# A transformer layer with eight experts: the matmuls of each expert get three widths chosen at run time, some adds of the prefix-sum step move to GpSimd, and the routing step gets a second buffer

## The reference, cut to what matters

```python
# attention part: prefix sums over time, no softmax
k_real = xn @ Wk;  v = xn @ Wv
k = exp(1j * 10 * k_real);  rotors = exp(1j * t * freqs)
out = gate0 * real(cumsum(v * rotors) * conj(rotors)) / sqrt(t + 1)
    + gate1 * real(cumsum(v * conj(k shifted by one token)) * k) / sqrt(t + 1)
attn = out @ Wo
# expert part: every token goes to the one expert with the largest probability
probs = softmax(xn @ gate_w);  e = argmax(probs)
ffn = probs[e] * (gelu(xn @ w1[e] + b1[e]) @ w2[e] + b2[e])      # 1024 -> 4096 -> 1024
```

## Time and profile before

| | |
|---|---|
| median of 3 runs | 1149.34 us (1148.93 to 1155.68) |
| the profiled execution | 1152.25 us; its slowest core's span 1150.4 us |
| spans of the eight cores | 1135.3 to 1150.4 us, the longest is core 4 |
| busy on core 4 | PE 932.1, PEld 611.9, DVE 756.4, ACT 598.4, POOL 162.6 us |
| instructions on core 4 | 18743 |
| HBM read, written by core 4 | 321.18 MB, 17.90 MB |

### The profile page before, as it was taken

How to read it: one execution, slowest core, us unless ns; L and a number is a source line. 1 busy time by engine, 2 the same in 40 slices (tenths; PEclk the granted TensorE clock), 3 DMA queues, 4 the chain that set the end, 5 groups by cost and what they waited for, 6 DMA issues and landing times.

```text
span 1150.4 us, 18743 instructions; the slowest of 8 cores (1135.3 to 1150.4 us)
## 1 busy us (share of the span) xinstructions
PE 932.1 (81%) x6221; PEld 611.9 (53%) x6296; DVE 756.4 (66%) x1909; ACT 598.4 (52%) x1014; POOL 162.6 (14%) x184
## 2 busy tenths in 40 slices
PE   3756689699989999988889978987898784978592
PEld 2323456465656666656556646654665462544261
DVE  4726444756645546689976998999989995321331
ACT  4354477668875795576347634873377422210000
POOL 0000121001112111121012101210121110311101
PEclk9876689999989999999899988998899887988896
DMA  8999999995999999999999999999999999999982
GB/s 190 228 204 205 203 158 172 163 158 106 164 139 160 181 179 162 159 174 169 159 176 170 169 156 175 173 163 159 159 164 167 158 156 196 210 230 217 203 230 79
DMA packets 123779, 199.69 MB, mean 174 GB/s; under 512 B 4755, under 2 KB 70691, under 8 KB 123680
## 3 DMA queue, kind: packets, MB, share of 16 engines
q0 software_dynamic: 107056, 151.65, 88.8%
q1 hardware_dynamic: 16624, 46.80, 12.6%
HBM read 321.18 MB, written 17.90 MB: 295 GB/s over the span
## 4 chain that ended last, share of the span: by engine, by line
PE 33%; DVE 22%; issue 18%; DMA 18%; ACT 7%; POOL 1%; DVEq 1%; SPq 0%; ACTq 0%; POOLq 0%
PE yb L935 10%; DMA yg<-ys,gidx 10%; PE wb L621 9%; PE wb L880 8%; DVE pp L723 6%; DMA ring<-w 5%; PE yb L406 3%; DVE pp L729 2%; DVE pp L726 2%; DVE pp L749 1%; DVE pp L677 1%; DVE m L655 1%; PE wb L582 1%; DVE st L340 1%; DMA resf<-xown 1%
## 5 line engine op out<-in xcount | busy, mean ns | idle before, releaser
L880 PE MATMUL wb<-xsT,ring 128*128 128x288 bf16 x2048 | 275.4, 293 | 32.1 <-DMA ring<-w 14.6
L935 PE MATMUL yb<-hT,ring 128*128 128x288 bf16 x2048 | 283.3, 294 | 18.7 <-ACT yT L950 16.5
L880 PEld LDWEIGHTS wb<-xsT,ring 128*128 128x128 bf16 x2048 | 202.6, 100 | 100.7 <-issue 37.2
L935 PEld LDWEIGHTS yb<-hT,ring 128*128 128x128 bf16 x2048 | 204.0, 100 | 90.5 <-issue 26.7
L315 POOL DMA_DIRECT2D ring<-w x128 | 106.1, 832 | 778.9 <-PE yb L935 381.1
L890 ACT ACTIVATE hT<-wb,cfs 128x288 bf16<-128x288 f32 x256 | 118.5, 501 | 100.9 <-PE wb L880 100.1
L650 ACT ACTIVATE cs<-cs 128x512 f32<-128x512 f32 x64 | 40.3, 630 | 116.4 <-DVE cs L644 115.9
L667 DVE COPY cs<-bnd 128x2 f32<-128x2 f32 x64 | 11.1, 173 | 135.1 <-ACT cs L652 134.1
L621 PE MATMUL wb<-xT,wks 128*128 128x512 bf16 x339 | 87.1, 398 | 12.3 <-ACT hT L890 9.7
L621 PE MATMUL wb<-xT,wvs 128*128 128x512 bf16 x383 | 93.0, 386 | 0.1
L723 DVE TENSOR_TENSOR_SCAN pp<-pp,cpos,one 128x256 f32<-128x256 f32 x128 | 88.9, 736 | 3.8 <-DVE pp L729 0.5
(11 more groups left out here) (151 smaller groups left out, 1288.4 us busy)
## 6 DMA issues: line engine op xcount, KB each, us to landing
ring<-w POOLq DMA_DIRECT2D x128, 1024.0 KB, 22.1
xt<-xown SPq DMA_DIRECT2D x16, 512.0 KB, 8.2
xt<-xfh SPq DMA_DIRECT2D x16, 512.0 KB, 10.0
resf<-xown SPq DMA_DIRECT2D x16, 512.0 KB, 13.6
out<-resf SPq DMA_DIRECT2D x16, 512.0 KB, 9.1
xr<-xnb SPq DMA_DIRECT2D x16, 256.0 KB, 9.6
yg<-xr SPq DMA_DIRECT2D x16, 256.0 KB, 7.6
ys<-xsr SPq DMA_DIRECT2D x7, 576.0 KB, 10.6
```

The source lines that it names most:

```text
L880: fn = lambda e, kt=kt, b=b, a=a, k=k: e.matmul(b[:, 0:CAP], ring[k][:, (kt % 4) * DM + a * P:(kt % 4) * DM + (a + 1) * P], xsT[:, kt * CA ...
L935: fn = lambda e, d=d, kc=kc, k=k: e.matmul(yb[d][:, 0:CAP], ring[k][:, (kc % 8) * CH + d * P:(kc % 8) * CH + (d + 1) * P], hT[:, kc * CAP: ...
```

## The change

PE gets three copies of each expert's whole stretch of instructions (the units between the matmuls included), which differ only in the columns of the L880 and L935 matmuls: 256, 272 or 288. Ahead of the stretch PE loads the expert's token count into a register and branches. ACT and all other engines keep working on 288 columns; `yb` is cleared once so that columns never written hold numbers. In the prefix-sum step the second half of `pp` becomes two alternating buffers `pa`, two adds (L749, L751) go to POOL, the two kinds of scan change order and the rotation of the carry takes two DVE operations and not four. In the preparation `xn32` gets a second buffer that lies over ring slots 4 and 5, ACT's copy of the router product is issued one tile later, the last two groups share one copy, and the normalisation of two tiles moves ahead of the last router products.

```diff
+WIDTHS = [256, 272, CAP]
+    def ways(self, choose, *toks):
+        self.q.append((toks, choose, "ways", 0))
+    def meet(self):
+        self.q.append(((), None, "meet", 0))
...
+            if sem == "ways":
+                end = next(k for k in range(at, len(queue)) if queue[k][2] == "meet")
+                fn(eng, lambda: self.emit(eng, queue[at:end], dict(seen)))
...
+    def by_width(e_):
+        def choose(e, emit):
+            if not regs:
+                regs.append(e.alloc_register("width"))
+            e.reg_load(regs[0], cnt[0:1, e_:e_ + 1])
+            def at(k):
+                width[0] = WIDTHS[k]
+                if k + 1 == len(WIDTHS):
+                    emit()
+                    return
+                with e.If_lt(regs[0], WIDTHS[k] + 1):
+                    emit()
+                with e.Else():
+                    at(k + 1)
+                e.end_ifs()
+                width[0] = CAP
+            at(0)
+        return choose
...
     def stage1(e_, at_ct):
+        if e_ in wayed:
+            T.ways(by_width(e_), t_gi[0])
...
-                        b[:, 0:CAP],
+                        wide(b),
...
         hT_free[0] = t_m
+        if e_ in wayed:
+            T.meet()
...
+    for b in yb:
+        V.op(lambda e, b=b: e.memset(b[:], 0.0))
...
+        V.op(lambda e: e.tensor_scalar(
+            cnt[:], b4[:, 0:NE], 0.0, None, ALU.add), t_p)
...
-    def rotate(j, re, im, t):
-        V.op(lambda e: e.tensor_scalar(m2[:, 2:3], im, sa(j), None, ALU.mult), t, t_al2[0])
-        t2 = V.op(lambda e: e.tensor_scalar(m2[:, 3:4], re, nsa(j), None, ALU.mult))
-        V.op(lambda e: e.scalar_tensor_tensor(
-            cpos[:, 2 * j:2 * j + 1], re, ca(j), m2[:, 2:3], ALU.mult, ALU.add), t2)
+    def rotate(j, x, t):
+        V.op(lambda e: e.tensor_tensor(m2[:, 2:4], x, sab(j), ALU.mult), t, t_al2[0])
         return V.op(lambda e: e.scalar_tensor_tensor(
-            cpos[:, 2 * j + 1:2 * j + 2], im, ca(j), m2[:, 3:4], ALU.mult, ALU.add))
+            cpos[:, 2 * j:2 * j + 2], x, ca(j), ap(m2, 3, [[4, P], [-1, 2]]),
+            ALU.mult, ALU.add), (V.sem, V.n))
...
+        t_b = V.op(lambda e: e.tensor_tensor(a3, v3, bind, ALU.mult), t, added.get(s - 2))
...
+        t_g = G.op(lambda e: e.tensor_tensor(A[:, 0:CH], A[:, 0:CH], A[:, CH:2 * CH], ALU.add), t2)
...
-        z_t[(c, j)] = V.op(lambda e: e.tensor_tensor(
+        added[s] = z_t[(c, j)] = G.op(lambda e: e.tensor_tensor(
             ap(z[c], j * CH, [[KT * CH, P], [LR, 2], [1, LR]]), q2(0),
-            ap(pp, 2 * CH, [[W, P], [LR, 2], [1, LR]]), ALU.add), t2)
+            ap(A, 0, [[2 * CH, P], [LR, 2], [1, LR]]), ALU.add), t1, t_g)
...
-            turning = group(i - 1)
+            summed = group(i - 1)
...
-        if i0 + n in (4, 8, 12):
-            xn32_free[0] = t_l
+        xn32_free[i0 // 4 % 2] = t_l
...
+    fh_norm(0, 1)
+    group(14)
+    turn_logits(*take_logits(12, 4, slice(0, CH), group(NLT - 1)[3]))
```

More of the change, by code:

```diff
@@ L60, in dma, with emit @@
         return (slot.sem, slot.n)
+    def ways(self, choose, *toks):
+        self.q.append((toks, choose, "ways", 0))
+    def meet(self):
+        self.q.append(((), None, "meet", 0))
     def run(self, eng):
-        seen = {}
-        for toks, fn, sem, step in self.q:
+        self.emit(eng, self.q, {})
+    def emit(self, eng, queue, seen):
+        at = 0
+        while at < len(queue):
+            toks, fn, sem, step = queue[at]
+            at += 1
             for tok in toks:
@@ L68, in run @@
                     eng.wait_ge(tok[0], tok[1])
+            if sem == "ways":
+                end = next(k for k in range(at, len(queue)) if queue[k][2] == "meet")
+                fn(eng, lambda: self.emit(eng, queue[at:end], dict(seen)))
+                at = end + 1
+                continue
             ins = fn(eng)
@@ L125, in build_program @@
             for i in range(NRES)]
-    ring = []
-    ring_off = at[0]
+    ring, ring_off = [], at[0]
     for k in range(NRING):
@@ L130, in build_program @@
     hT, hT_off = sb("hT", NCT * CAP, BF16)
-    xn32 = sb("xn32", KT * CH, F32, hT_off)[0]
+    xn32 = [sb("xn32%d" % k, KT * CH, F32, o)[0]
+            for k, o in enumerate((hT_off, ring_off + 8192 * (NRING - 2)))]
     xsT, xsT_off = sb("xsT", KT * CAP, BF16)
@@ L407, in logits @@
                 b[0:NE, c], gws[:, kt * NE:(kt + 1) * NE],
-                xn32[:, kt * CH + c.start:kt * CH + c.stop],
+                xn32[i0 // 4 % 2][:, kt * CH + c.start:kt * CH + c.stop],
                 start=(kt == 0), stop=(kt == KT - 1))
@@ L711, in outs @@
         W = 4 * CH
+        A = pa[s % 2]
         p3 = ap(pp, 0, [[W, P], [CH, 2], [1, CH]])
@@ L880, in stage1 @@
                     fn = lambda e, kt=kt, b=b, a=a, k=k: e.matmul(
-                        b[:, 0:CAP],
+                        wide(b),
                         ring[k][:, (kt % 4) * DM + a * P:(kt % 4) * DM + (a + 1) * P],
-                        xsT[:, kt * CAP:(kt + 1) * CAP], start=(kt == 0), stop=(kt == KT - 1))
+                        wide(xsT[:, kt * CAP:(kt + 1) * CAP]), start=(kt == 0), stop=(kt == KT - 1))
                     if a == 7 and kt == 3:
@@ L935, in stage2 @@
                     fn = lambda e, d=d, kc=kc, k=k: e.matmul(
-                        yb[d][:, 0:CAP],
+                        wide(yb[d]),
                         ring[k][:, (kc % 8) * CH + d * P:(kc % 8) * CH + (d + 1) * P],
-                        hT[:, kc * CAP:(kc + 1) * CAP], start=(kc == 0), stop=(kc == NCT - 1))
+                        wide(hT[:, kc * CAP:(kc + 1) * CAP]), start=(kc == 0), stop=(kc == NCT - 1))
                     if kc == NCT - 1 or (d == 3 and kc % 8 == 7):
@@ L957, in stage2 @@
         hT_free[0] = t_m
-    yd_t = {}
+        if e_ in wayed:
+            T.meet()
+    yd_t, wayed = {}, set(range(NE))
     og_t = [None, None]
@@ L1142, in more @@
         yb_free[:] = [None] * 4
-        for x in (h_t, yT_t, yr_t, yTr_t, ring_tok, rf_t, out_t, yg_t):
+        for x in (h_t, yT_t, yr_t, yTr_t, ring_tok, rf_t, out_t, yg_t, added):
             x.clear()
```

88 lines of the change are left out of this document (48 added, 40 removed).

## The result

| | before | after |
|---|---|---|
| median, measured side by side | 1152.51 us | 1258.01 us (1252.62 to 1298.33) |
| ratio to before, 95% interval | | 1.0903 [1.0851, 1.0955] |
| span of core 4 | 1150.4 us | 1243.5 us |
| longest span | 1150.4 us (core 4) | 1250.7 us (core 2) |
| mean granted clock of the cores | 0.907 to 0.912 | 0.861 to 0.874 |

The longest of the changed kernel's executions, 1298.33 us, had the four cores of one die at a lower granted clock (0.767 to 0.785), and the ratio leaves it out.

A forecast was written before the change was run, and what follows sets the result against it. Bound by PE in experts 0 and 1, DVE and ring in 3 to 6, in-order waits in preparation, transfers in expert 7. 1152.25 - 11 + 8 - 5 - 3 = 1141.3, for the median 1138 us; range 1112 to 1163.

The forecast's parts named there:

- 3 x 3.46 + 0.5 - 2.0: Border from 272 to 288 columns: three far jumps and a register load, less time hidden by queued matmuls, cost 8.9 us.
- The dear-jumps rival: Jumps cost double with DMA full: five in experts 0 to 2, 3.5 us more each, 1156 us; chance 0.12.
- PE's slack and the ring's backlog cover the jumps: From expert 3 on, 14 us of PE slack an expert and queued transfers hide the jumps; uncovered, 8.9, 2, 2, 2, 2 us.
- There PE is busy for 111.1 of 120 us, so PE sets the pace: Experts 0, 1 and half of 2: PE is the limit, so narrower matmuls save 5 us there.
- 12.4 forecast: DVE's output unit falls from 14.31 to 12.4 us by moved adds and shorter rotations; gain in experts 3 to 6: 5 us.
- The ports rival: POOL and DVE disturb each other: 2 x 1.4 us of adds stretch DVE, unit 15.2 us, 1172 us; chance 0.06.
- I take 0: Ring loads listed behind POOL's first add wait up to a unit; pieces in line hide that, cost 0.
- The rival: POOL's queue starves the ring in experts 5 and 6: DMA empty 2 us in 16 units, 1175 us; chance 0.10.
- The prediction's own sign: Ring: wrong if pieces come faster than 6.8 us, landing times drop below 10 us, or PE's branches are short.
- Ring as limit in experts 3 to 6: Ring, about 113 us an expert, holds beside DVE, so relieving DVE gains only 5 us, ends 0 and 9.
- the elastic-DMA rival: Experts 3 to 6: only DVE held and DMA can go faster, -45 us and not -5, 1098 us; chance 0.08.
- That rival (0.09): Preparation is transfer bound: nothing of the 11 us gain comes, 1149 us; chance 0.09.

The follow-up runs named there:

- e13: Kernel before with three 288-column copies, first always taken (one far jump an expert), and half the rows of the ring's loads left out in experts 3 to 6; 1164.49 us.
- e7: Kernel before with branches and three copies all at 288 columns, the first always taken: one far jump at each expert's end; 1178.76 us.
- e3: Kernel before with the new preparation alone; 1142.37 us, ratio 0.9996.
- e4: Kernel before with the branches and the three copies of 256, 272 and 288 columns alone; 1204.68 us, ratio 1.0546.
- e9: Kernel before with 256 columns in every expert matmul and no branch, leaving out tokens past an expert's 256th; 1138.5 us, ratio 0.9971.
- e10: As e2, with two additions left out in every output unit; 1123.27 us, ratio 0.9836.
- e2: Changed kernel without branches (288 columns throughout) and with both adds back on DVE; 1135.84 us, ratio 0.9928.
- e5: As e2, with a one-column POOL operation in the place of each add, with the same waits; 1185.29 us, ratio 1.0376.
- e12: As e2, with the load of Wv listed behind the gather of expert 0's tokens; 1130.46 us, ratio 0.9894.

## Why the prediction was wrong, point by point

- **The branches: count right, price wrong, cover wrong.** The 13 far jumps came where they were counted (272 one in and one out, 288 two in, 256 one out). The 2.0 us that queued matmuls hide at a border were near as well: 2.2 us at 503.3, 3.2 us at 258.3 (PE's last matmul ends at 261.49). The step that failed is "3 x 3.46 + 0.5 - 2.0": 3.46 us was read from the one row that there was the earlier trace rows, and that row lies at the program's end, after the transfers. In the changed kernel it is 6.4 us on average (e13 shows the traffic as a cause). The dear-jumps rival had this price at 0.12, but took over the second failed step, that from expert 3 on PE's slack and the ring's backlog cover the jumps. In e7 each of experts 3 to 6 with its border is 2 to 9 us longer than before, 23 us for four jumps of 28.4 us together, and against e3 33 us; in e4 it is 15 and 25. So little or nothing was covered. The clock adds to a stop: in e7 it is 0.50 from 619.3 to 626 us, behind the jump at 611.7, and the prediction had charged its 2 us for this to one stop alone. That the 14 us of slack an expert of the earlier trace rows are small pauses in a chain of DVE, ring and PE, and not a reserve at the border, is my reading and not shown. Where two or three jumps come in a row next to nothing is hidden: the two borders from 272 to 288 cost e4 17 and 25 us, where 8.9 was forecast for the first and nothing for the second. Nor did core 4 stay the slowest; core 2, with 12 jumps, is.
- **The narrower matmuls: worth far less than their columns.** "There PE is busy for 111.1 of 120 us, so PE sets the pace" gave 5 us for a small part of the columns. e9 took all of them, 54 us, and gained 3.4. In its core 4 trace experts 0, 1 and 2 are 4, 4 and 2 us shorter than before, half of the 20.4 us saved there, but from expert 0's start to expert 7's e9 takes 805 us and e3 809, so 4 us are left of it. So PE set the pace there in part only, and a busy share of 0.93 was no proof of more.
- **DVE's unit: 12.4 forecast, 14.9 measured.** The unpriced term was the two engines side by side. The adds gone from DVE save 1.56 us (e10 against e2), and the stretched operations (1.04 and 1.08 us) take more than that back. The ports rival had the mechanism and nearly the unit (15.2) at a chance of 0.06; its price in time was 29 us for the unit, where the estimate above makes 17. The 1.4 us for a POOL add were fair (1.26), but this add was called free because "the buffers give the next unit most of its own length": it is the add's effect on its neighbour that counts, not its result's due time.
- **The rotation: halved in count, no gain.** A rotation takes 0.37 us and not 0.69 (707.42 to 707.79 in e2's DVE timeline), yet the unit of e2 is 14.37 against 14.31.

```profile
641.53 1.28 DVE L744 SCALAR_TENSOR_TENSOR pp<-pp,cfs,cs 128x1024 f32<-128x1024 f32 x1
642.72 0.68 DVE L748 TENSOR_TENSOR pp<-pp 128x512 f32<-128x512 f32 x1
...
707.42 0.13 DVE L686 TENSOR_TENSOR m<-pp,al 128x2 f32<-128x2 f32 x1
707.65 0.22 DVE L687 SCALAR_TENSOR_TENSOR cpos<-pp,al,m 128x2 f32<-128x2 f32 x1
707.79 0.68 DVE L674 SCALAR_TENSOR_TENSOR cs<-cs 128x512 f32<-128x512 f32 x1
...
711.12 1.28 DVE L773 SCALAR_TENSOR_TENSOR pa<-pa,cfs,cs 128x1024 f32<-128x1024 f32 x1
712.51 0.69 DVE L776 TENSOR_TENSOR pa<-pa 128x512 f32<-128x512 f32 x1
```

The first two of these rows are before's product and what follows it. There L744 to L748 goes start to start in 1.19 us, and L748 doesn't need L744. In the new order these operations need the one just before them, and L773 to L776 takes 1.39 us. "Reordered scans cost nothing, being the same instructions" was the failed step; that this order is the cause was read from the trace and not tried.
- **POOL's queue: "I take 0".** It cost 49 us in e5, the larger part of what the adds cost. The rival had the mechanism, and gave it experts 5 and 6 alone, since four pieces stand in line in 3 and 4. e5's line is thinner from expert 3 on (0.97 and 151 GB/s from 473 us): a line of four pieces is there because POOL issues at once when a slot comes free, and the first held-back load ends it. The prediction's own sign came too: it called itself wrong if landing times dropped below 10 us, and from 500 to 1029 us the least is 8.9 us and the median 14.9, where the earlier trace rows had medians of 28.2 and 17.6. Wo, which no term and no rival named, is behind the same waits.
- **Ring as limit in experts 3 to 6: right in kind, too tight in size.** 50 us less of DVE gave 12.6 us over the kernel, where 5 (0 to 9) was forecast for these experts; in core 4's traces they take 439 us in e10 and 459 in e2. Most of the time still went nowhere, and the elastic-DMA rival (45 us) is out. (The stretch is 464 us by the table, and not the 451 of the prediction.)
- **Preparation: worked-out step right, limit wrong.** The routing's matmuls came 18 us earlier in e3 (at 105.56 and not 123.4 us) and expert 0 started 4 us earlier. The prediction said "the transfers don't all follow", but I took 11 of 15 by the window's mean of 206 GB/s; the transfer that held was one gather behind 8 MB in one queue. That rival (0.09) was right: nothing of the 11. e12 shows that part of the gain was there.
- **Expert 7: 3 us, nothing came.** At its start PE idles 14.4 us in e2, where the earlier trace rows had 14.66. In the changed kernel PE waits 18.7 us for Wo in expert 7.
- **The chances.** 0.17 for slower was spread over three mechanisms as if at most one would come. None of them had its price in a row of before (the earlier trace rows shows a jump without traffic), all three lie in what the change adds, and all three came: 62 us for the branches and 66 for the adds, against the 8 that e2 gained.

## What to carry to other kernels

A term that no row prices and that I set at nothing needs the cost it would have without its cover, multiplied by how often it happens; here 32 units and 13 jumps made each small one large. When work is moved to an engine that also issues transfers, count what is listed behind its waits before counting its busy time: an engine at 14% busy is no free engine. And read a duration beside the state it was taken in: a jump measured after the transfers have ended is not the jump in the middle of them.

## What was not expected of the hardware

- The same far jumps of PE take 3.4 to 4.4 us at a DMA share of 0.53 to 0.65 and 6.8 to 7.7 us at a full one (e13, e7); the longest seen in the changed kernel was 8.96 us. The page counts 77 packets in the instruction queue, before 53.
- A DVE operation on two numbers that meets a POOL add of 512 f32 columns lasts as long as the add (0.22 to 1.26 us).
- A stop of 21.86 us at a border was followed by a granted clock of 0.50, and 24 matmuls took twice their time.
- The Trainium skill, Advanced Engine Details and Errata, "Engine Queue Depths", with its 64 entries for TensorE, had made a larger cover likely. At the border from expert 2 to 3 PE ran on for 2.2 us after the first jump began, at the one from 0 to 1 for 3.2 us; the 2.0 from the earlier trace rows was nearer than the prediction's 3.9, an estimate from the 64 entries of the Trainium skill.
